# Moving rotation and weight splitting between VectorE and GpSimd at the start of a fused attention and feed-forward kernel

## The reference

```python
x = x + attn(layernorm(x), wq, wk, wv, wo)      # 16 query heads, 4 key/value heads, 128 wide
x = x + ffn(layernorm(x), W1, W2, W3)
# attn: q = rope(x wq), k = rope(x wk), v = x wv; the inputs are regrouped as
#       sequences; linear attention with a decay exp(-lam * (i - j)) for j <= i,
#       no softmax; o wo
# ffn:  fwht(silu(x W1) * (x W3)) W2             # fwht: Walsh-Hadamard transform of 1024
```

## Time and profile before

| what | value |
|---|---|
| median of 3 runs | 271.09 us (270.62 to 271.42) |
| span of the profiled execution | 269.5 us |
| median less this span | 1.6 us |
| busy in the span: PE, PEld | 261.0 us, 227.4 us |
| busy in the span: DVE, ACT, POOL | 204.9 us, 167.7 us, 143.9 us |
| granted TensorE clock | 1.000 throughout |

### The profile page before, as it was taken

The page is one execution under the profiler, slowest core; times in us unless marked ns, Lnnn a source line. Parts: engine busy times, 40 slices in busy tenths (PEclk is TensorE's granted clock), DMA queues, the critical chain, the costliest instruction groups (busy, mean ns, idle before and its releaser), DMA issues.

```text
span 269.5 us, 4222 instructions
## 1 busy us (share of the span) xinstructions
PE 261.0 (97%) x1506; PEld 227.4 (84%) x1506; DVE 204.9 (76%) x336; ACT 167.7 (62%) x283; POOL 143.9 (53%) x105
## 2 busy tenths in 40 slices
PE   7898799999999999999999999999999999999995
PEld 5786488979889888888889889898888879988895
DVE  4799899899979897869899799795575984143333
ACT  3879896875898767556867768984353542043230
POOL 2302989888889467532795897899519200000000
DMA  6594620211220000000020001200000000100002
GB/s 205 189 346 169 243 80 2 78 31 47 80 78 4 0 1 0 4 0 0 2 61 17 2 11 67 80 2 2 0 0 2 0 0 21 59 0 2 0 0 78
DMA packets 5635, 13.23 MB, mean 49 GB/s; under 512 B 624, under 2 KB 2544, under 8 KB 5616
## 3 DMA queue, kind: packets, MB, share of 16 engines
q1 hardware_dynamic: 5040, 12.39, 13.4%
q10 hardware_dynamic: 576, 0.59, 0.6%
HBM read 11.93 MB, written 1.05 MB: 48 GB/s over the span
## 4 chain that ended last, share of the span: by engine, by line
PE 72%; DVE 15%; ACT 5%; issue 4%; DMA 2%; POOL 1%; SPq 0%; DVEq 0%; ACTq 0%
PE bank L317 24%; PE bank L318 24%; PE bank L319 23%; DVE rope_b L1014 2%; DVE rope_a L1013 2%; DMA w_raw<-in_wq 2%; DVE bank L1041 2%; DVE v_hid L1000 1%; PE bank L333 1%; ACT rope_b L661 1%; ACT rope_b L660 1%; DVE qk L1021 1%; DVE rope_b L1065 1%; DVE o_lo L1051 1%; DVE p_lo L1046 1%
## 5 line engine op out<-in xcount | busy, mean ns | idle before, releaser
L843 POOL TENSOR_TENSOR qk<-rope_a,rope_b 128x512 f32<-128x512 f32 x36 | 49.7, 1383 | 25.6 <-DVE rope_b L1014 25.1
L317 PE MATMUL bank<-xt_hi,w_hi 128*128 128x512 f32 x140 | 55.0, 393 | 0.5 <-issue 0.4
L318 PE MATMUL bank<-xt_lo,w_hi 128*128 128x512 f32 x140 | 54.7, 391 | 0.0
L319 PE MATMUL bank<-xt_hi,w_lo 128*128 128x512 f32 x140 | 54.5, 389 | 0.0
L850 POOL TENSOR_TENSOR q_hid<-qk,q_hid 128x512 fp32r<-128x512 f32 x29 | 39.8, 1379 | 10.4 <-ACT q_hid L666 10.4
L673 ACT ACTIVATE p_hi<-bank 128x512 fp32r<-128x512 f32 x48 | 28.6, 596 | 15.7 <-DVE bank L1041 15.2
L1014 DVE TENSOR_TENSOR rope_b<-rope_b,sin_sb 128x512 f32<-128x512 f32 x40 | 37.7, 942 | 0.0
L318 PE MATMUL bank<-w_lo,o_hi 128*128 128x256 f32 x128 | 36.2, 283 | 0.0
L319 PE MATMUL bank<-w_hi,o_lo 128*128 128x256 f32 x128 | 36.2, 283 | 0.0
L317 PE MATMUL bank<-w_hi,o_hi 128*128 128x256 f32 x128 | 36.1, 282 | 0.0
L1013 DVE TENSOR_TENSOR rope_a<-bank,cos_sb 128x512 f32<-128x512 f32 x40 | 27.5, 687 | 10.6 <-ACT rope_b L661 10.1
(11 more groups left out here) (90 smaller groups left out, 614.8 us busy)
## 6 DMA issues: line engine op xcount, KB each, us to landing
w_raw<-in_w SPq DMA_DIRECT2D x6, 512.0 KB, 3.2
decay_sb<-in_decay SPq DMA_DIRECT2D x4, 512.0 KB, 5.3
w_raw<-in_wo SPq DMA_DIRECT2D x4, 512.0 KB, 4.7
w_raw<-in_wq SPq DMA_DIRECT2D x3, 512.0 KB, 3.3
x_sb<-in_x SPq DMA_DIRECT2D x3, 256.0 KB, 7.1
out<-x_sb SPq DMA_DIRECT2D x6, 128.0 KB, 1.8
w_raw<-in_wv SPq DMA_DIRECT2D x1, 512.0 KB, 6.1
w_raw<-in_wk SPq DMA_DIRECT2D x1, 384.0 KB, 6.4
```

What stands on the lines that cost most here:

```text
L317: pe.matmul(o, a_hi, b_hi, start=first, stop=False, skip_group_check=shared)
L318: pe.matmul(o, a_hi, b_lo, start=False, stop=False, skip_group_check=shared)
L319: return pe.matmul(o, a_lo, b_hi, start=False, stop=last, skip_group_check=shared)
L843: pool.tensor_tensor(qk[:, r % 2, :], rope_a[:, r % 2, :], rope_b[:, r % 2, :], ALU.add).then_inc(rope_sum_pool, 1)
```

## The change

The first four units' lists are changed, and the number of raw buffers:

- Four raw buffers in place of three; SP issues chunk 3 without waiting for the first low parts, and a load waits for the low part of the chunk four places before.
- The low part of chunk 3 (wq) goes from DVE to POOL, that of chunk 2 (wk, now all 1024 columns) from POOL to DVE, behind p_lo of unit 0's second tile. ACT makes the high part of chunk 3 ahead of that of chunk 2 (`HIGH_ORDER`).
- Sum and low part of Q2 (the third query) go from DVE to POOL.
- On DVE both remaining masks of unit 0 and the first `low_p` go ahead of the rotation of Q3 (the fourth).
- On POOL the low part of chunk 4 goes behind the low part of Q3.
- On ACT the first two `high_p` go ahead, between the swaps, and chunk 4's high part goes behind the swap of Q4.

```diff
-SLOTS = 3
+SLOTS = 4
-LOW_ON_DVE = (0, 3, 5, 7)
+HIGH_ORDER = (0, 1, 3, 2) + tuple(range(4, len(CHUNKS) - 2))
+LOW_ON_DVE = (0, 2, 5, 7)
-SUM_ON_DVE = (0, 1, 2, 3)
-ROPE_LOW_ON_DVE = (0, 1, 2, 3)
+SUM_ON_DVE = (0, 1, 2)
+ROPE_LOW_ON_DVE = (0, 1, 2)
@@ SP
             load_chunk(2)
-            sp.wait_ge(first_lo, len(FIRST))
             load_chunk(3)
@@ ACT
             high_v(0, 3)
+            high_weights(3)
+            swap(("Q", 0, 2))
+            high_p(0, S_FIRST0)
             high_weights(2)
-            swap(("Q", 0, 2))
-            high_weights(3)
+            swap(("Q", 0, 3))
+            high_p(0, S_SECOND)
+            high_rope(("Q", 0, 2))
+            swap(("Q", 0, 4))
             high_weights(4)
-            swap(("Q", 0, 3))
-            high_rope(("Q", 0, 2))
-            high_p(0, S_FIRST0)
-            high_p(0, S_SECOND)
-            swap(("Q", 0, 4))
             high_rope(("Q", 0, 3))
@@ low_weights, on POOL and on DVE
-                wait_ge(w_hi_done, n + 1)
+                wait_ge(w_hi_done, HIGH_ORDER.index(n) + 1)
@@ POOL
             low_weights(1)
-            low_weights(2)
+            low_weights(3)
+            rope_add(("Q", 0, 2))
+            low_rope(("Q", 0, 2))
             rope_add(("Q", 0, 3))
+            low_rope(("Q", 0, 3))
             low_weights(4)
-            low_rope(("Q", 0, 3))
             rope_add(("Q", 0, 4))
@@ DVE
             mask(0, S_FIRST0)
             rotate(("Q", 0, 2))
-            low_weights(3)
-            rope_add(("Q", 0, 2))
-            rotate(("Q", 0, 3))
-            low_rope(("Q", 0, 2))
             mask(0, S_SECOND)
             mask(0, S_FIRST1)
             low_p(0, S_FIRST0)
+            rotate(("Q", 0, 3))
             low_p(0, S_SECOND)
+            low_weights(2)
             tile_stats(1, 0)
```

More of the change, by code:

```diff
@@ L854, in low_weights @@
                 a = FIRST_OF.get(n, 0)
-                pool.wait_ge(w_hi_done, n + 1)
+                pool.wait_ge(w_hi_done, HIGH_ORDER.index(n) + 1)
                 pool.tensor_tensor(w_lo[:, at + a:at + CH], w_raw[:, n % SLOTS, a:],
@@ L979, in low_weights @@
                 _, _, at = CHUNKS[n]
-                dve.wait_ge(w_hi_done, n + 1)
+                dve.wait_ge(w_hi_done, HIGH_ORDER.index(n) + 1)
                 dve.tensor_tensor(w_lo[:, at:at + CH], w_raw[:, n % SLOTS, :], w_hi[:, at:at + CH].bitcast(F32),
```

## The result

| kernel | median | ratio to before, 95% interval |
|---|---|---|
| before, four runs | 270.86 us (270.59 to 271.42) | 1 |
| changed, four runs | 273.2 us (273.12 to 273.31) | 1.0088 (1.0076 to 1.0100) |

A forecast was written before the change was run, and what follows sets the result against it. PE runs unbroken after 56 us; before it, full, ordered DVE bounds. The 0.8 us won at the first attend is lost again, K1 adds 2.9: span 269.5 to 272.4, plus 1.6 for the median gives 274.0 us, range 270.9 to 275.4.

The forecast's parts named there:

- The walk: Step-by-step forecast over the engines' four queues; o_lo of the first pair 2.9 us late, carried to the end.
- The tie of step 3: POOL's low part of Q2 and DVE's rope_b of Q3 forecast 0.02 us apart; POOL first was assumed.
- the case of 2.9 us: POOL's low part of Q2 goes ahead of DVE's rope_b of Q3: 2.9 us late, 274.0 us.
- that of 3.6: DVE's rope_b of Q3 goes first; chunk 2's w_lo then holds back Q3's sum to 30.8: 3.6 us, 274.7 us.
- Step 7: POOL's sum of Q4 ends at 36.4, or 37.5 if DVE's chunk 5 goes first; before, 33.8.
- Forecast (d): POOL's backlog at chunk 4 makes the sum of Q4 late: 274.0 us (273 to 275), chance 0.66.
- A sign of being wrong: The prediction is wrong if PE's pauses between 32 and 56 us together stay under 1 us.
- Rival (a): DVE alone is the bound and its 1.2 us lighter load comes out at the end: 269.9 us, chance 0.11.
- Rival (b): Holds between DVE and POOL are not paid as charged: 271.3 us, within 0.5; chance 0.15.
- Rival (c): Early loads push the chain at 9.3 us back, on top of the walk: upper bound 275.6 us, chance 0.08.
- The cover: Chunk 6's late landing at 34.2 is hidden by the late sum of Q4 (36.4): cost 0, without it 0.7 us.

The follow-up runs named there:

- e2: Changed kernel with POOL's low part of chunk 4 moved behind the sums of Q4 and Q5: 273.07 us, ratio 1.0079.
- e7: Kernel before with only POOL's low part of chunk 4 moved behind the low part of Q3: 273.33 us, ratio 1.0086.
- e9: e6 with the low part of chunk 4 on DVE instead of POOL: 270.95 us, ratio 1.0004.
- e3: Changed kernel with SP's wait before chunk 3 put back, four raw buffers kept: 273.17 us, ratio 1.0083.
- e8: Kernel before with only the sum and low part of Q2 moved from DVE to POOL: 271.15 us, ratio 1.0005.
- e1: Kernel before with only the fourth raw buffer and without SP's wait: 270.73 us, ratio 0.9995.
- e5: e2 with POOL's subtraction for chunk 4 replaced by two clears that read nothing from SBUF: 272.41 us, ratio 1.0055.
- e6: Changed kernel with the exchange of chunks 2 and 3 undone, low and high parts: 271.99 us, ratio 1.0039.
- e12: e11 with chunk 7's low part on DVE moved from behind K2's rotation to behind Q11's: 273.85 us, ratio 1.0104.
- e11: Kernel before with unit 2's third-tile and first-output low parts on DVE ahead of Q9's rotation: 270.86 us, ratio 0.9999.

## Why the prediction was right, and where it was off

The direction, the place and the holds, step by step, came as forecast. The cause that the sum named, and one of the signs given for being wrong, did not. The walk against the trace of the changed kernel, whose times are moved by 0.59 us:

| step | forecast | measured + 0.59 |
|---|---|---|
| 1 rope_b of Q2 ends | 24.15 | 24.16 |
| 2 projection of Q5 | 26.6 | 26.61 |
| 3 low part of Q2 on POOL starts | 26.46 | 26.44 |
| 3 rope_b of Q3, issued / ends | 26.48 / 28.3 | 26.48 / 28.27 |
| 3 first attend | 29.0 | 28.93 |
| 4 sum of Q3 ends | 29.7 | 29.63 |
| 5 chunk 2's w_lo ends | 30.8 | 30.72 |
| 5 K1's projection | 31.8 | 31.70 |
| 6 chunk 4 ends | 34.6 | 34.65 |
| 6 rope_b of Q5 ends | 35.15 | 35.20 |
| 7 sum of Q4 ends | 36.4 or 37.5 | 36.38 |
| 8 rope_a of K1 | 38.4 or 39.5 | 38.27 |
| 8 o_lo | 40.6 | 40.32 |

- **The tie of step 3** went to POOL, which was 0.04 us ahead (25.85 against 25.89), so the case of 2.9 us and not that of 3.6. The walk could not tell which; that the sum was built on the right case is in part luck.
- **Step 7**, who goes first when POOL waits and DVE has another two-operand instruction: POOL, which is the first of the two cases (w_lo of chunk 5 took 2.31 us, so the sum of Q4 was ahead of it).
- **The size.** 2.9 us became 2.6 at o_lo, in about equal parts: K1's rotation came 0.13 us sooner than in the walk, and its sine multiplication needed 1.44 us from its start to that of o_lo instead of 1.6, since POOL started the low part of Q4 at 38.54 and not at 38.8. Behind o_lo the walk carried everything on, and another 0.2 us came back in the multiplications of Q6 and Q7 (1.24 and 0.75 us, before 1.37 and 0.81): 2.4 at the end.
- **The cause that the sum named, and what the runs put in its place.** Forecast (d) made POOL's backlog, the late sum of Q4, the cause. e2 removed that wait and the time stayed. e7 shows that chunk 4's place alone is enough for the loss, and e9 that taking chunk 4 off POOL, with the exchange undone, removes it. What these kernels have in common in their traces is what the walk had priced at each step: the places where POOL's reads meet DVE's instructions with two SBUF operands.
- **A sign of being wrong that came.** The prediction was to be wrong if PE's pauses between 32 and 56 us stayed under 1 us together. They did: 0.74 us, all before the attend of unit 1, and none before the scores of the third pair, which stand behind it. The sign did not reckon with the clock. In the profiled execution six matmuls ran at the lower clock from 31.11 on and filled 1.2 us in which PE would have waited. e3 has the same work at a clock of 1.000 throughout, and PE pauses there for 1.86 us, with the same time at the end:

```profile
40.44 0.38 PE L318 MATMUL bank<-w_hi,o_hi 128*128 128x256 f32 x1 [0.37 <-DVE o_lo L1054]
...
43.62 0.50 PE L318 MATMUL bank<-p_hi,v_hid 128*128 128x512 f32 x1 [1.49 <-DVE p_lo L1049]
```

- **Rival (a)**, DVE's lighter load, fell with e8. **Rival (b)** had the holds at nothing; up to rope_b of Q5 the held instructions end within 0.1 us of the walk. **Rival (c)** fell with e1 and e3.
- **Chunk 6** landed late as forecast: ACT idled 0.45 us for it and was still early for the sum of Q4, which it awaited for 1.29 us more. The cover held:

```profile
33.44 1.06 ACT L625 ACTIVATE w_hi<-w_raw 128x1024 fp32r<-128x1024 f32 x1 [0.45 <-DMA w_raw<-in_wo]
35.79 0.63 ACT L666 ACTIVATE q_hid<-qk 128x512 fp32r<-128x512 f32 x1 [1.29 <-POOL qk L843]
```

What stays open: how much of the 2.4 us the holds make by themselves. By replacement this was shown at one place only (e5), where 0.66 us of a hold of 1.94 reached the end; for the rest it is the account in the first section, which adds up at o_lo but is an account and not a test. A kernel with all of POOL's reads made harmless wasn't tried.

## What to carry to other kernels

Here VectorE was full and GpSimd read SBUF beside it, and moving Q2's operations from one to the other was worth nothing by itself (e8), while the place of one GpSimd instruction was worth 2.3 us (e7). So ask for each long GpSimd instruction which VectorE instructions lie beside it, and put it beside those that read a PSUM bank or beside an idle stretch. A hold shows in no list of waits, only as a duration above the operation's own; so compare the busy sum of the engine with its instruction count first, and then look whether a wait behind the hold takes it up. And taking away one wait in a full, ordered queue is no gain until the next hold behind it has been looked for. Last, a sign that counts pauses of PE has to say at which clock.

## What the runs showed of the hardware

- In the meetings looked at, the waiting side went next, in both directions. A waiting DVE instruction passed POOL's next one (the earlier trace rows at 30.8), and a waiting POOL instruction passed DVE's next: in the changed kernel the sum of Q4, issued at 34.02, ran ahead of the w_lo issued at 34.53.
- POOL went first with a lead of 0.04 us (25.85 against 25.89), and with 0.01 us in e6 (33.79 against 33.80). No run shows the same queues with such a race the other way, so what it is worth is not shown.
- Not held beside POOL's w_lo of 28.46 to 30.83 in the kernel before: two p_lo and a rope_a, which read a bank (under 0.7 us each), and a bn_stats with one input (0.41 us).
- A small instruction was held as long as a large one: a DVE instruction on 4 columns took 2.34 us in e12 beside POOL's w_lo of 67.27 to 69.63, and 0.15 us in e11.
- The granted clock was 0.50 from 31 to 34 us in the changed kernel, the level of 1.2 GHz: six matmuls from 31.11, behind PE's pause of 1.46 us, took 0.63 us and more instead of 0.40, 1.2 us in all. The pause alone doesn't bring this about, for e3 has the same pause and stays at 1.000. It cost nothing, since PE paused for p_lo at 43.63 anyway: e3 takes 273.17 us and the changed kernel 273.2.
- In the kernel before, a lower clock does cost: beside the experiments, its executions at a mean of 0.993 or 0.994 took 271.27 to 271.86 us, the others 270.75 in the median. The loss is not one of the clock: at full clock e3 is still 2.4 us slower.

The second of the six matmuls at the lower clock, from PE's timeline of the changed kernel:

```profile
31.70 0.63 PE L318 MATMUL bank<-xt_lo,w_hi 128*128 128x512 f32 x1
```
